# A transformer block on one core: the order of two steps on GpSimd, and the output projection of the first chunk in three pieces

## The chip, the cores and the metric

The kernel runs on one core of one Trainium2 chip. The metric is the device time of one execution in microseconds; the lower the better. The engines are TensorE (PE), VectorE (DVE), ScalarE (ACT), GpSimd (POOL) and SyncE (SP, which here only issues DMAs). Each works through its own instructions in order and waits on semaphores for the others.

## The reference

One block of a diffusion transformer: 2 sequences of 2048 tokens, width 576, 16 heads of 36, hidden width 2304, all in float32.

```python
mod = swish(c) @ w_mod + b_mod
sh_msa, sc_msa, g_msa, sh_mlp, sc_mlp, g_mlp = split(mod, 6, axis=1)
xn = _ln(x) * (1 + sc_msa) + sh_msa
q, k, v = heads(xn @ w_qkv + b_qkv)
q, k = _ln(q, g_q), _ln(k, g_k)                 # over the 36 of a head
attn = softmax(q @ k.T * HD ** -0.5)
x = x + g_msa * (heads_joined(attn @ v) @ w_proj + b_proj)
xn2 = _ln(x) * (1 + sc_mlp) + sh_mlp
x = x + g_mlp * (gelu(xn2 @ w1 + b1) @ w2 + b2)
```

## The kernel before, in words

Products are split: a float32 operand is kept as a 16-bit high part and a 16-bit rest, and a product is the sum of three 16-bit ones.

**Attention.** The work is 8 groups `G` of 4 heads (4 groups for each sequence), each of 16 units `u`; `U = 16 G + u` counts them. A unit is one head and 512 queries, and has 8 steps `s` of 256 keys. In a step PE computes `scores` (L1183) into a PSUM pair, ACT takes the exponential (L755) into one of 4 buffers `p`, and three steps later PE multiplies by the values: `sums` (L1200, float32) for steps 0 to 3, `sums_high` (L1211) and `sums_low` (L1220) for steps 4 to 7. For those DVE first rounds `p` (`round_p`, L927) and forms the rest (`low_p`, L935). `scores` of step s waits for the exponential of step s - 2. So in step 3 of a unit, PE can't begin before ACT has done the exponential of step 1.

**Tiles of the next group.** While a unit is attended, the queries, keys and values of one tile (128 tokens) of the next group are made: PE multiplies 7 of the 14 products in step 0 and 7 in step 1 (`tile_products`, L1237). ACT squares the result in step 4 (L725), DVE sums the squares in step 5 (`tile_sum`, L895, L899), POOL takes the power -1/2 (`tile_power`, L623), and DVE scales by it at the start of the next unit (`tile_normal`, L903).

**Slices of the weights of groups 2 and 3.** The weights `w_qkv` of these two groups are centred and cut during groups 0 and 1. It is done in 6 slices for each of the two, slice `u - 1` in unit `u` = 1 to 6:
- DVE, step 3 of unit u: `sum_word` (L304, a sum for each head);
- POOL, unit u: `centre_word`, two instructions (L311 the mean, L313 the subtraction);
- ACT, unit u + 1, step 0, behind the exponential: `high_word` (L319; L321 and L322 for slice 4; L325 and L326 for slice 5);
- DVE, unit u + 1, step 2: `low_word` (L283).

POOL's loop over the units holds, in this order: `head` (in every fourth unit: copies of the values of the next head, L613, L614 and L616), `centre_word`, `tile_power` for tile U + 1.

**The last group.** In group 7 there is no next group. Its units have `scores` and `sums` only, and the MLP's first chunk of 512 tokens is begun in them. In units 9 to 12 PE multiplies the attention output of one tile each by `w_proj` (`tensor_early`, L1843): 14 products, each of two matmuls of 288 columns, into PSUM banks that nothing else uses there. `PROJECT_AT` says for each step which of the 14 are done in it. DVE takes the result in step 7 of the same unit (`gate_part`, L1731). After the attention come 8 chunks of the MLP (L1864, L1883, L1890), with PE on a fixed order.

Of the kernel before, what the change touches and what calls it, by code (L numbers as in the profile page):

```python
# [340 lines left out]
def split_products(xhi, xlo, w, tokens, cols, bias=True):  # L341

    for k in range(KF):
        yield xhi[:, k, tokens], w[:, k, cols]
        yield xhi[:, k, tokens], w[:, KF + k, cols]
        yield xlo[:, k, tokens], w[:, k, cols]
    yield xhi[:, KF, tokens], w[:, 8, cols]
    if bias:
        yield xlo[0:97, KF, tokens], w[0:97, 9, cols]
    else:  # L350
        yield xlo[:, KF, tokens], w[:, 8, cols]


def attention_mlp(nc, keep, place, x, c, w_mod, b_mod, w_qkv, b_qkv, g_q, g_k, b2, sums_dram, den_dram, rden_dram, mods_dram, out, halves,
# [3 lines left out]
    with ExitStack() as ctx:  # L358
# [3 lines left out]
        TILES = (GROUPS - 1) * NT  # L362
# [111 lines left out]
        def _(sp):  # L474
# [6 lines left out]
            def turn_heads(m):  # L481
                t, i0, i1, _, n = PARTS[m]
                sp.wait_ge(low_ready, m + 1)
                sp.wait_ge(high_ready, 2 * m + 2)
                for i in range(i0, i1):
                    sp.dma_start_transpose(qk_even[:, :, (t * TPC + i) * P:(t * TPC + i + 1) * P],  # L486
                                           stk[:, t % 2, i, :, :].rearrange("p e n -> p (e n)")).then_inc(tq_stored[n], 16)
# [113 lines left out]
        def _(pool):  # L601
            def head(Hh):

                part, h, a = (Hh // GH) % 2, Hh % GH, Hh % 2
                if Hh == 0:
                    pool.wait_ge(raw_ready, RAWS)
                    pool.wait_ge(v_blank, 1)
                else:
                    pool.wait_ge(exp_done, (Hh * NCH - 1) * STEPS + 3)
                if Hh >= 2:  # L610
                    pool.wait_ge(low_p_used, (Hh - 1) * NCH * SPLITS)
                rows = v32[:, part * NT + 2 * SPLIT[0]:part * NT + 2 * SPLIT[-1] + 2, h, :]
                pool.tensor_copy(vr[:, a, :, 0:RW], rows).then_inc(v_high, 1)  # L613
                pool.tensor_copy(v16[:, a, :, :], rows)  # L614
                pool.wait_ge(v_high, Hh + 1)
                pool.tensor_tensor(vr[:, a, :, HP:HP + HD], rows[:, :, 0:HD], vr[:, a, :, 0:HD].bitcast(F32), ALU.subtract).then_inc(head_ready, 1)  # L616

            def tile_power(X):
                if X in EPS_BY_POOL:
                    pool.wait_ge(t_ssq, X + 1)  # L620
                    pool.tensor_tensor(tssq[:, 1, :], tssq[:, 0, :], keep.head_eps[:, 0:QK], ALU.add).then_inc(t_msq, 1)
                pool.wait_ge(t_msq, X + 1)
                pool.tensor_tensor(tssq[:, 1, :], tssq[:, 1, :], keep.power[:, 0:QK], ALU.pow).then_inc(t_rstd, 1)  # L623
# [51 lines left out]
            for U in range(GROUPS * UNITS):  # L675
                G, u = U // UNITS, U % UNITS
                if U == RSTD_IN * UNITS:
                    pool.wait_ge(n_mv, NT + 1)
                    pool.tensor_tensor(nrstd[:, 0, :], nmv[:, :, 1], keep.eps[:, 0:1].broadcast_to([P, NT]), ALU.add).then_inc(n_var, 1)
                    pool.wait_ge(n_var, 1)  # L680
                    pool.tensor_tensor(nrstd[:, 1, :], nrstd[:, 0, :], keep.power[:, 0:NT], ALU.pow).then_inc(n_rstd, 1)
                if (G in HAT_GROUPS and u == 0) or (G == HATS_IN and u == LATE_FROM):
                    n = 2 if G > HATS_IN else int(u == LATE_FROM)
                    pool.wait_ge(n_rows, 16 * (1, 3, 4)[n])
                    if n < 2:
                        pool.memset(hat_lo[n][:, H:KC * P], 1.0)
                    pool.tensor_scalar(scale_row[n], scale_row[n], 1.0, None, ALU.add).then_inc(n_hole, 1)
                if u % NCH == NCH - 1 and U + 1 < SPLIT_UNITS:
                    head(U // NCH + 1)
                if start.slice_at(G, u):  # L690
                    start.centre_word(pool, *start.slice_at(G, u))
                if U + 1 < TILES:
                    tile_power(U + 1)
                if G == GROUPS - 1:
                    rest.gpsimd_early(pool, u)
            rest.gpsimd(pool)
# [700 lines left out]
class Mlp:  # L1397
# [6 lines left out]
    TILES = (B * NG - 1) * NT  # L1404
# [5 lines left out]
    SUMS_AT = {2: 2, 4: 3, 5: 4}  # L1410
    HIGH_IN = MULTIPLY_IN
    PROJECT_IN = {9 + i: i for i in range(TPC)}
    PROJECT_AT = (None, (0, 14), None, None, None, None, None, None)
    NORMAL_IN = {10 + i: i for i in range(TPC)}
    TURN_IN = 14
    TURN_AT, AFFINE_AT, LOW_X_AT = ({s: k for k, s in enumerate(at)} for at in ((0, 1, 3, 4, 6), (1, 2, 4, 5, 7), (2, 3, 5, 6)))
# [412 lines left out]
    def tensor_early(self, pe, u, s):  # L1829
        if u in self.PROJECT_IN and self.PROJECT_AT[s]:  # L1830
            i, (n0, n1) = self.PROJECT_IN[u], self.PROJECT_AT[s]
            ops = list(split_products(self.ohi, self.olo, self.wp, slice(i * P, (i + 1) * P), slice(0, H)))
            if n0 == 0:
                if i == 0:
                    pe.wait_ge(self.olo_ready, KC)
                    pe.wait_ge(self.wp_loaded, 16 * 7)
                    pe.wait_ge(self.ends.t_yn, self.TILES + 1)
                else:
                    pe.wait_ge(self.pair_taken, i)
            for n in range(n0, n1):  # L1840
                l, w = ops[n]
                for half in range(2):
                    last = self.nc.tensor.matmul(self.early_pair[:, half, :], l, w[:, half * HALF:(half + 1) * HALF],  # L1843
                                                 start=(n == 0), stop=(n == len(ops) - 1))
            if n1 == len(ops):
                last.then_inc(self.pair_ready, 1)
        if u == self.TURN_IN and s in self.TURN_AT:
            if s == 0:
                pe.wait_ge(self.pair_taken, TPC)
            self.turn_y(pe, 0, (self.TURN_AT[s],))  # L1850
# [155 lines left out]
```

## Time and profile before

| | |
|---|---|
| median of 3 runs | 2650.73 us (2650.32 to 2651.53) |
| profiled execution | 2651.53 us, of which 2649.7 are the span |
| granted clock of PE | 0.999 |
| busy: PE, DVE, ACT, POOL | 99%, 62%, 55%, 18% |
| a unit in groups 0 to 6 | 12.46 us |
| a unit in group 7, without and with a projection | 10.35 and 14.01 us |

The span is from the first to the last instruction; the time also holds what lies around it. A share of busy time is an average over stages that differ: what a change is worth depends on who waits for whom in its own stage. The starts of instructions on POOL are more to be trusted than their durations.

### The profile page before, as it was taken

The numbers are of one execution on the slowest core, as the hardware profiler recorded it, in microseconds if no ns is written. First come the engines' busy times: TensorE is split into PE (matmuls) and PEld (weight loads), VectorE is DVE, ScalarE is ACT, GpSimd is POOL, SyncE is SP. The second block draws the span as 40 slices with busy tenths as digits, with TensorE's granted clock in tenths as the row PEclk, the third lists the DMA queues.
The fourth block names the chain that finished last, engine by engine and source line by source line (L and its number), as shares of the span: only waits on it lengthen the run. The fifth ranks groups of instructions, "written<-read, shape, count | busy, mean of one in ns | idle before, by whom it ended". The sixth has DMA issues, their size and how long they took to land.

```text
span 2649.7 us, 42010 instructions
## 1 busy us (share of the span) xinstructions
PE 2611.8 (99%) x15820; PEld 1318.7 (50%) x15820; DVE 1647.1 (62%) x2677; ACT 1467.4 (55%) x2174; POOL 469.4 (18%) x339
## 2 busy tenths in 40 slices
PE   6999999999999999999999999999999999999999
PEld 3444444444444444444444334375757575666657
DVE  7788887788888788888888512344343535353421
ACT  4787787777777788788788786412121211111110
POOL 2532332222222222222222100110101010010100
PEclk9999999999999999999999999999999999999999
DMA  7513311133332123333333322402020211202000
GB/s 234 95 36 79 79 36 35 46 74 72 69 73 50 46 70 81 73 78 81 78 79 84 99 77 91 157 15 96 18 79 26 70 60 37 72 24 84 13 19 19
DMA packets 257862, 179.10 MB, mean 68 GB/s; under 512 B 172745, under 2 KB 211087, under 8 KB 256953
## 3 DMA queue, kind: packets, MB, share of 16 engines
q1 hardware_dynamic: 257370, 176.37, 25.0%
q8 instruction: 125, 2.05, 0.3%
q14 instruction: 79, 0.65, 0.1%
q10 hardware_dynamic: 288, 0.04, 0.0%
HBM read 96.49 MB, written 41.06 MB: 52 GB/s over the span
## 4 chain that ended last, share of the span: by engine, by line
PE 94%; DMA 1%; DVE 1%; SPq 1%; ACT 1%; issue 1%; POOL 0%; DVEq 0%; ACTq 0%
PE at_ps L1864 19%; PE at_ps L1200 18%; PE at_ps L1183 17%; PE at_ps L1890 14%; PE at_ps L1237 11%; PE at_ps L1211 8%; PE at_ps L1220 4%; PE at_ps L1883 1%; PE at_ps L1826 1%; PE at_ps L1843 1%; DMA ml_held<-head_rden 1%; PE at_ps L1261 1%; PE at_ps L1918 0%; DMA st_wm_first<-in_L_cond_b_mod 0%; SPq L486 0%
## 5 line engine op out<-in xcount | busy, mean ns | idle before, releaser
L755 ACT ACTIVATE at_p<-at_ps 128x1024 f32<-128x1024 f32 x1024 | 1040.0, 1029 | 330.9 <-PE at_ps L1183 326.3
L1200 PE MATMUL at_ps<-at_p,at_v 128*37 128x512 f32 x2304 | 590.3, 592 | 0.0
L935 DVE TENSOR_TENSOR at_rest_of_p<-at_p,at_pr 128x1024 bf16<-128x1024 f32 x448 | 553.0, 1234 | 15.4
L623 POOL TENSOR_TENSOR at_tssq<-at_tssq,power 128x8 f32<-128x8 f32 x112 | 276.7, 2470 | 880.6 <-DVE at_tssq L899 879.9
L1864 PE MATMUL at_ps<-ml_w2s,ml_hid 128*128 128x288 f16 x3348 | 414.9, 286 | 0.0
L1890 PE MATMUL at_ps<-ml_xhi,ml_w 128*128 128x512 f16 x1296 | 382.0, 379 | 0.0
L1864 PEld LDWEIGHTS at_ps<-ml_w2s,ml_hid 128*128 128x128 f16 x3348 | 327.5, 98 | 82.0
L1211 PE MATMUL at_ps<-at_pr,at_vr 128*101 128x512 f32 x896 | 365.1, 489 | 1.3 <-DVE at_pr L927 1.2
L927 DVE CAST at_pr<-at_p 128x1024 fp32r<-128x1024 f32 x448 | 314.6, 702 | 81.0 <-ACT at_p L755 78.9
L1183 PE MATMUL at_ps<-at_qk_even 109*64 109x512 f16 (+1 forms) x1536 | 308.7, 382 | 3.8 <-ACT at_p L755 2.6
L1183 PE MATMUL at_ps<-at_qk_odd 109*64 109x512 f16 (+1 forms) x1658 | 308.6, 381 | 0.3 <-ACT at_p L755 0.3
L1237 PE MATMUL at_ps<-at_wq,at_xhi 128*128 128x432 f16 x1008 | 295.9, 348 | 0.0
L1653 ACT ACTIVATE ml_g<-at_ps,ml_b1col 128x512 f32<-128x512 f32 x144 | 95.9, 685 | 351.5 <-PE at_ps L1883 244.4
L1731 DVE TENSOR_TENSOR ml_part<-at_ps,ml_gates 128x576 f32<-128x576 f32 x63 | 47.7, 757 | 360.0 <-PE at_ps L1864 333.8
L1183 PEld LDWEIGHTS at_ps<-at_qk_odd 109*64 109x64 f16 (+1 forms) x1658 | 96.9, 107 | 256.0 <-issue 217.6
L1636 ACT ACTIVATE ml_aff<-at_ps,cols 128x512 f32<-128x512 f32 x40 | 31.0, 775 | 348.0 <-PE at_ps L1826 348.0
L1890 PE MATMUL at_ps<-ml_xlo,ml_w 128*128 128x512 f16 x576 | 218.3, 379 | 0.0
L1183 PEld LDWEIGHTS at_ps<-at_qk_even 109*64 109x64 f16 (+1 forms) x1536 | 92.2, 106 | 244.6 <-issue 194.9
L1890 PEld LDWEIGHTS at_ps<-ml_xhi,ml_w 128*128 128x128 f16 x1296 | 123.4, 98 | 158.1 <-issue 16.2
L1200 PEld LDWEIGHTS at_ps<-at_p,at_v 128*37 128x37 f32 x2304 | 134.8, 114 | 119.5 <-issue 1.9
L1237 PE MATMUL at_ps<-at_wq,at_xlo 128*128 128x432 f16 (+1 forms) x560 | 193.9, 346 | 0.0
L1787 DVE CAST ml_hid<-ml_g 128x512 f16<-128x512 f32 x144 | 61.2, 425 | 205.0 <-ACT ml_g L1653 205.0
(189 smaller groups left out, 2365.3 us busy)
## 6 DMA issues: line engine op xcount, KB each, us to landing
head_sums<-at_oT SPq DMA_DIRECT2D x256, 72.0 KB
ml_held<-head_sums SPq DMA_DIRECT2D x64, 256.0 KB
at_xy<-in_L_cond_w SPq DMA_DIRECT2D x34, 288.0 KB
w_halves<-at_wq SPq DMA_DIRECT2D x68, 144.0 KB
at_xy<-in_x SPq DMA_DIRECT2D x32, 288.0 KB, 2.8
ml_x<-in_x SPq DMA_DIRECT2D x8, 1152.0 KB, 5.4
out<-ml_x SPq DMA_DIRECT2D x7, 1152.0 KB, 4.5
ml_held<-head_rden SPq DMA_DIRECT2D x24, 216.0 KB
```

Source lines behind the costliest of these rows:

```text
L623: pool.tensor_tensor(tssq[:, 1, :], tssq[:, 1, :], keep.power[:, 0:QK], ALU.pow).then_inc(t_rstd, 1)
L755: act.activation(p[:, s % NP, :], ps[:, 2 * (s % 2):2 * (s % 2) + 2, :].rearrange("p a n -> p (a n)"), ACT.Exp).then_inc(exp_done, 1)
L927: nc.vector.tensor_copy(pr[:, n % NZ, :], p[:, s % NP, :]).then_inc(rounded, 1)
L935: nc.vector.tensor_tensor(rest_of_p[:, n % NL, :], p[:, s % NP, :], pr[:, n % NZ, :].bitcast(F32), ALU.subtract).then_inc(low_p_ready, 1)
L1183: last = nc.tensor.matmul(ps[c:c + keys, 2 * (s % 2) + a, :], qk[0:SW, GH + h, key:key + keys], qk[0:SW, h, qc * CH:(qc + 1) * CH], start= ...
L1200: last = nc.tensor.matmul(acc[a * HP:a * HP + RW, bank_of(U)], v32[:, (G % 2) * NT + 2 * s + a, h, :], p[:, s % NP, a * CH:(a + 1) * CH], ...
L1211: last = nc.tensor.matmul(acc[0:VW, bank_of(U)], vr[:, Hh % 2, 2 * k + a, :], pr[:, n % NZ, a * CH:(a + 1) * CH], start=False, stop=False, ...
L1220: last = nc.tensor.matmul(acc[a * HP:a * HP + RW, bank_of(U)], v16[:, Hh % 2, 2 * k + a, :], rest_of_p[:, n % NL, a * CH:(a + 1) * CH], st ...
L1237: last = nc.tensor.matmul(tile_bank(X, 0, 3 * GW), l, rhs[:, g * 3 * GW:(g + 1) * 3 * GW], start=(n == 0), stop=(n == count - 1))
L1653: act.activation(self.g32[:, f % 2, :], self.up_bank(f), ACT.Gelu_apprx_tanh, bias=self.b1col[:, f:f + 1], scale=1.0 / WS).then_inc(self.g ...
L1864: last = nc.tensor.matmul(self.pair(i)[:, half, :], l, w[:, half * HALF:(half + 1) * HALF], start=(n == 0), stop=(n == len(ops) - 1))
L1890: last = nc.tensor.matmul(self.up_bank(f), w, xs, start=first and n == 0, stop=not first and n == len(ops) - 1)
```

## The change

It has two parts that have nothing to do with each other. On POOL, `tile_power` of a unit stands ahead of `centre_word` of the same unit, where it stood behind. `PROJECT_AT` gives 5, 5 and 4 of the 14 products to steps 1, 2 and 3, where it gave all of them to step 1.

```diff
                 if u % NCH == NCH - 1 and U + 1 < SPLIT_UNITS:
                     head(U // NCH + 1)
+                if U + 1 < TILES:
+                    tile_power(U + 1)
                 if start.slice_at(G, u):
                     start.centre_word(pool, *start.slice_at(G, u))
-                if U + 1 < TILES:
-                    tile_power(U + 1)
                 if G == GROUPS - 1:
                     rest.gpsimd_early(pool, u)
...
     PROJECT_IN = {9 + i: i for i in range(TPC)}
-    PROJECT_AT = (None, (0, 14), None, None, None, None, None, None)
+    PROJECT_AT = (None, (0, 5), (5, 10), (10, 14), None, None, None, None)
     NORMAL_IN = {10 + i: i for i in range(TPC)}
```

## Rows read from the trace of the kernel before

**Rows 1.** The page: the chain that ended last, by engine

```profile
PE 94%; DMA 1%; DVE 1%; SPq 1%; ACT 1%; issue 1%; POOL 0%; DVEq 0%; ACTq 0%
```

**Rows 2.** By stretch: length, busy PE, PEld, DVE, ACT, POOL, clock, DMA

```profile
111.13:211.00 99.87, 99.87 (x563) 42.82 (x561) 83.40 (x124) 79.98 (x121) 30.52 (x26) 1.00 0.23 52
...
1588.57:1644.50 55.93, 55.93 (x370) 24.95 (x368) 10.80 (x22) 34.15 (x37) 2.20 (x6) 1.00 0.34 107
```

**Rows 3.** Waits of PE's matmuls, 111.2 to 1500 us: total, times, longest

```profile
PE at_ps L1211 <- DVE at_pr L927: 1.2, 2, 0.7
PE at_ps L1183 <- ACT at_p L755: 0.3, 1, 0.3
```

**Rows 4.** The chain in order of time, unit 3: start, us, what

```profile
138.69 0.47 PE at_ps L1211 x2
139.16 1.29 PE at_ps L1237 x7
140.46 0.43 PE at_ps L1183 x2
```

**Rows 5.** Timeline of PE and ACT, units 3 and 6: start, us, [idle before]

```profile
141.28 0.62 PE L1183 MATMUL at_ps<-at_qk_even 109*64 109x512 f16 x4
...
137.45 0.56 ACT L319 ACTIVATE at_wq<-st_later 128x432 f16<-128x432 f32 x1
138.73 1.02 ACT L755 ACTIVATE at_p<-at_ps 128x1024 f32<-128x1024 f32 x1 [0.71 <-PE at_ps L1183]
140.93 1.02 ACT L755 ACTIVATE at_p<-at_ps 128x1024 f32<-128x1024 f32 x1 [1.17 <-PE at_ps L1183]
...
175.40 0.56 ACT L322 ACTIVATE st_later<-st_later 64x432 f16<-64x432 f32 x1
176.10 1.02 ACT L755 ACTIVATE at_p<-at_ps 128x1024 f32<-128x1024 f32 x1
```

**Rows 6.** Timeline of POOL: units 0 to 3

```profile
110.77 1.64 POOL L623 TENSOR_TENSOR at_tssq<-at_tssq,power 128x8 f32<-128x8 f32 x1 [6.77 <-DVE at_tssq L899]
119.94 0.73 POOL L311 TENSOR_SCALAR st_lone_mean<-st_lone 128x8 f32<-128x8 f32 x1 [7.53 <-DVE st_lone L304]
120.76 1.60 POOL L313 TENSOR_TENSOR st_later<-st_later,st_lone_mean 128x288 f32<-128x288 f32 x1
...
131.99 0.25 POOL L311 TENSOR_SCALAR st_lone_mean<-st_lone 128x8 f32<-128x8 f32 x1 [4.64 <-DVE st_lone L304]
132.32 0.67 POOL L313 TENSOR_TENSOR st_later<-st_later,st_lone_mean 128x288 f32<-128x288 f32 x1
137.31 2.52 POOL L623 TENSOR_TENSOR at_tssq<-at_tssq,power 128x8 f32<-128x8 f32 x1 [4.32 <-DVE at_tssq L899]
139.41 0.68 POOL L613 CAST at_vr<-at_v 128x296 fp32r<-128x296 f32 x1
```

**Rows 7.** Timeline of DVE: units 1 and 2

```profile
119.88 0.69 DVE L927 CAST at_pr<-at_p 128x1024 fp32r<-128x1024 f32 x1
...
132.34 1.20 DVE L927 CAST at_pr<-at_p 128x1024 fp32r<-128x1024 f32 x1 [0.44 <-ACT at_p L755]
...
139.10 0.69 DVE L927 CAST at_pr<-at_p 128x1024 fp32r<-128x1024 f32 x1
139.82 1.34 DVE L935 TENSOR_TENSOR at_rest_of_p<-at_p,at_pr 128x1024 bf16<-128x1024 f32 x1
```

**Rows 8.** Timeline of ACT and PE at the start of the attention

```profile
100.61 2.84 ACT L755 ACTIVATE at_p<-at_ps 128x1024 f32<-128x1024 f32 x3
...
102.59 0.62 PE L1183 MATMUL at_ps<-at_qk_even 109*64 109x512 f16 x4 [0.23 <-ACT at_p L755]
```

**Rows 9.** The chain in order of time: group 7, and a long run of the MLP

```profile
1589.86 3.54 PE at_ps L1843 x28
1593.40 0.55 PE at_ps L1183 x4
...
1765.01 13.23 PE at_ps L1864 x108
```

## The prediction

> **What bounds the kernel now.** I read the page first, then the busy times by stretch, then the chain of work that ended last in the two places that the change touches, and last the timelines of ACT, DVE and POOL there. The page gives PE 94% of the chain that ended last [rows 1]. That is a mean over the whole span, so the two stages come next: in the first 100 us of the group 0 stage PE is busy in all of its 99.87 us, and in the part of group 7 with the projections in all of 55.93 [rows 2]. A matmul's end is modelled, so I don't take this alone. The table of waits says the same from the other side: from 111 to 1500 us a matmul waited 1.2 us for DVE and 0.3 us for ACT, all told [rows 3]. The chain through unit 3 shows no piece that isn't PE, and each piece begins where the last ended [rows 4]. So whatever holds PE up in these stages is added to the time in full, and nothing that only lightens ACT, DVE or POOL is worth anything.
>
> **Part A: the order on POOL.** In units 1 to 6 of groups 0 and 1, POOL now runs `centre_word` and then `tile_power`; afterwards it is the other way round. Twelve slices of weights are centred there. No instruction is added. What matters is what each waits for. `centre_word` waits for DVE's sum of step 3 (L304); `tile_power` waits for DVE's L899, which comes in step 5 and, since DVE runs behind, only after ACT has begun the next unit. Behind `centre_word` waits ACT's `high_word`, in step 0 of the next unit and ahead of the exponentials of steps 1, 2 and so on.
>
> Take unit 3 (PE's step 1 block at 139.16). Its slice was centred from 131.99 to 132.99, and ACT took it at 137.45 [rows 5, 6]: 4.5 us to spare. Turned round, the centring can't start before the power is through, and the power started at 137.31, only 0.14 us before ACT wants the result. POOL's next instruction after it starts 2.10 us later (139.41 after 137.31) [rows 6]; I use this spacing, not the recorded 2.52 us.
>
> - A small gain first. The DVE rounding of step 4 (L927) takes 1.20 us when the centring (L313 at 132.32) falls on it and 0.69 us otherwise [rows 6, 7]. With the centring moved away, L899 and the power come 0.50 us earlier: 137.31 becomes 136.81.
> - Where the centring lands: 2.10 us after the power's start. DVE then runs the rounding of step 7 (L927, from 1.79 to 2.48 us after that start) and the subtraction L935 (from 2.51) [rows 7]. One case of this kind is in the trace, the first slice: L311 started 0.06 us into an L927, took 0.73 us instead of 0.25, and L313 after it took 1.60 instead of 0.67 [rows 6, 7]. From the end of the L927 (120.57) to the end of L313 (122.36) it took 1.79 us. So I take 2.48 + 1.79 = 4.27 us after the power's start: the slice is centred at 141.08.
> - ACT: 0.05 us for the semaphore (estimate, from the 0.04 us between the end of the scores at 138.69 and the exponential at 138.73 [rows 4, 5]), 0.70 us for `high_word` with what follows it (the same 0.56 us activation at 175.40 has the exponential behind it at 176.10 [rows 5]), then the exponential of step 1, 1.02 us: it ends at 142.85 where it ended at 139.75.
> - PE: `scores` of step 3 waits for that exponential. It started at 141.28. An ACT end reaches PE in about 0.06 us (exponentials from 100.61, the second of three ends near 102.53, matmul at 102.59 [rows 8]). So it starts at 142.91: PE stands still for 1.63 us.
>
> From the second stalled unit on there is 0.19 us more. From the exponential of step 2 to that of step 4 ACT works without a gap. Before, the exponential of step 2 started 0.35 us ahead of PE's scores of step 3 (140.93, 141.28 [rows 5]). After a stall it starts 0.10 us ahead of the end of the step 1 exponential (three in a row overlap by 0.10 each: 2.84 us, not 3.06 [rows 8]), and the scores 0.06 behind that end, 0.16 apart: ACT is 0.19 us later against PE. DVE's L899 follows the exponential of step 4, and so the next power. That gives 1.82 us. For the last two slices of a group `high_word` is two activations of 0.56 us [rows 5], so 2.38 us. A group: 1.63 + 3 x 1.82 + 2 x 2.38 = 11.85 us; two groups 23.7 us. Nothing later gives this back, since PE is the chain from there on. The rest that hangs on it has cover: the head's copies on POOL come behind the centring in one unit, but are wanted only in step 7 of the next, and `low_word` on DVE waits for the exponential of step 2, which ends later than `high_word`.
>
> The trace gives both ends of this cost. Below: if the centring runs freely 2.10 us after the power (0.32 from L311 to L313, and 0.67 for it [rows 6]: 3.09 instead of 4.27), each stall is 1.18 us shorter: 0.45, 0.64, 1.20, or 9.5 us in all. Were the power as short as the one of 1.64 us in unit 0 [rows 6], another 0.46 us goes and the sum is 4.0 us. Above: without the 0.50 us gain on DVE it is 29.7 us. I take 23.7, because the one slice of the trace that starts inside an L927 behaved so, and 2.10 lies 0.3 us inside that window at either side.
>
> The Trainium skill (SBUF — State Buffer, Who interferes with whom) states that a DVE instruction in a two-port mode, or with two SBUF inputs against a GpSimd instruction that reads SBUF, shares a port pair with GpSimd, that whoever issues first holds it for the whole instruction, and that the other blocks. The stretched pairs of [rows 6, 7] agree with this. By issue order alone L313, 2.42 us after the power, would come 0.09 us ahead of L935 at 2.51 and run freely, which is the sum of 9.5 us; with L311 first held by the L927, it is the sum of 23.7 us.
>
> **Part B: the projection in three pieces.** In units 9 to 12 of group 7, 14 products of two matmuls each stood in step 1; now 5, 5 and 4 stand in steps 1, 2 and 3. The matmuls are the same 112. ACT gets no new scores during the long block, but PE is the bound: it is busy throughout this stretch [rows 2], and no piece of its chain is late [rows 9]. The block takes 3.54 us, of which 28 x 0.1225 = 3.43 are its matmuls, by the rate of the same form in a long run, 13.23 us for 108 [rows 9]; the scores behind it take 0.55 us and not the 0.43 that they take in a chain without a change [rows 4, 9]. So entering and leaving a block costs 0.11 + 0.12 = 0.23 us. Eight more entries cost 1.8 us. Bounds: nothing, if the 7-product blocks of the earlier groups are the model, with scores of 0.43 us behind them [rows 4], to 2.6 us, if a block costs 0.33. The shorter gap on ACT is worth nothing, as no matmul waited for it. The result is read by DVE in step 7; after step 3 it still is there in time, four steps ahead.
>
> **Sum.** The profiled execution took 2651.53 us: 2649.7 of span and 1.8 around it. It is the slowest of the three; the median is 2650.73. 2651.5 + 23.7 + 1.8 = 2677.0, and by the median 2676.2. I forecast 2676.5.
>
> **Rivals.**
> - *The centring runs freely* (9.5 us in A): 2650.7 + 9.5 + 1.8 = 2662. For it: L313 would start 0.09 us ahead of L935. Against it: L311 starts inside an L927. Chance 0.15.
> - *More than that*: the stall feeds itself, or the 0.50 us don't come: 2650.7 + 29.7 + 1.8 = 2682 and beyond. For it: DVE is busy 83% of this stretch [rows 2]. Against: by the working above DVE has no new wait. Chance 0.13, a third of it above 2684.
> - *Nothing happens*, because ACT has more slack than I count or power and centring overlap: 2651 to 2653. The exponential of step 1 waited 0.71 us [rows 5] and the scores of step 3 stand 1.5 us behind its end, a slack of some 2.2 us against a lateness of 3.7. Chance 0.04.
> - *Faster*: if ACT never has to wait for the centring, the 0.50 us of DVE in 12 units would be the one effect, and would shorten the time where DVE sets the pace: 12 x 0.50 = 6 us less, 2650.7 - 6.0 + 1.8 = 2646.5. It decides from the point where the centring ends before ACT's 137.45 and PE waits for DVE; PE waited for DVE 1.2 us in 1400 [rows 3]. Chance 0.02.
>
> **How the numbers follow.** The forecast has 0.66, so some 0.94 lie on the slower side by more than 0.2% (5.3 us, about what can be told from no change here). The rival of 9.5 us and B come to 11.3 us, beyond that; the lowest bound, 4.0 and B, comes to 5.8. Same: 0.04; faster: 0.02. The range takes in the freely running centring and the sum without the DVE gain: 2661 to 2684.
>
> **What the profile after would show.** Right: the matmuls of step 3 (L1183) in units 2 to 7 and 18 to 23 wait for ACT, some 1.6 to 2.4 us each, 12 times, where none did; `high_word` (L319 and its neighbours) waits for POOL L313, some 3.7 us; L311 and L313 come after the power with 0.7 and 1.6 us; units there take 14.1 to 14.8 us and not 12.46; L927 of step 4 is 0.69 us. In group 7 three blocks of some 1.3, 1.3 and 1.1 us stand in each unit with a projection, each with scores of 0.55 us behind it and no wait of PE; the unit is 0.46 us longer. Wrong: L313 at 0.67 us and stalls near 0.6 us (the first rival), stalls that grow from slice to slice (the second), or ACT's L319 with no wait (the third). A granted clock below 1.00 in the stalled units would add what I haven't counted; it was 1.00 in both stretches [rows 2].

## The result and the profile after

The changed kernel takes 2684.51 us (median of 4 runs, 2684.31 to 2687.15), the kernel before takes 2651.13 us beside it (2650.32 to 2653.14, 4 runs). The ratio is 1.0127, with a 95% interval of 1.0109 to 1.0145: 33 us slower. The direction is as forecast. The time is 8 us above the forecast of 2676.5 and 0.5 us outside the range of 2661 to 2684. The profiled execution took 2684.21 us, 2682.4 of them span, at a mean granted clock of 0.996 (before: 2649.7 and 0.999).

The chain that ended last, by engine, over the whole span after the change:

```profile
PE 87%; issue 5%; POOL 2%; DVE 2%; DMA 1%; ACT 1%; SPq 1%; DVEq 0%; POOLq 0%; ACTq 0%
```

It was 94% of PE before [rows 1]. The 5% of "issue" are a sign of the new loop: where PE stands still the chain goes back over POOL, from one power to the next.

**Where PE waits.** The table of waits of the kernel after: first PE's, from 111 to 436 us (groups 0 and 1 where slices are centred), then ACT's behind POOL. The columns are what waited, for what, the microseconds in all, how many times and the longest.

```profile
PE at_ps L1183 <- ACT at_p L755: 23.0, 12, 2.5
...
ACT at_wq L319 <- POOL st_later L313: 32.0, 8, 4.1
...
ACT at_wq L321 <- POOL st_later L313: 7.8, 2, 4.1
ACT at_wq L325 <- POOL st_later L313: 7.4, 2, 3.7
```

There are twelve stalls of the scores, as forecast; before, PE had waited 0.3 us for ACT in 1400 us [rows 3]. Behind them `high_word` waits for the centring twelve times, some 4 us each. So the place and the mechanism of part A are there.

**One stalled unit.** The timeline of unit 3 (start, duration, engine, line; in brackets the idle time before and what ended it), on POOL, DVE, ACT and PE, to be read beside [rows 5 to 7]:

```profile
138.96 2.52 POOL L623 TENSOR_TENSOR at_tssq<-at_tssq,power 128x8 f32<-128x8 f32 x1 [9.73 <-DVE at_tssq L899]
141.56 1.23 POOL L311 TENSOR_SCALAR st_lone_mean<-st_lone 128x8 f32<-128x8 f32 x1
142.88 0.67 POOL L313 TENSOR_TENSOR st_later<-st_later,st_lone_mean 128x288 f32<-128x288 f32 x1
...
134.49 0.69 DVE L927 CAST at_pr<-at_p 128x1024 fp32r<-128x1024 f32 x1 [0.44 <-ACT at_p L755]
...
141.47 1.23 DVE L935 TENSOR_TENSOR at_rest_of_p<-at_p,at_pr 128x1024 bf16<-128x1024 f32 x1
...
143.58 0.56 ACT L319 ACTIVATE at_wq<-st_later 128x432 f16<-128x432 f32 x1 [4.05 <-POOL st_later L313]
144.05 1.92 ACT L755 ACTIVATE at_p<-at_ps 128x1024 f32<-128x1024 f32 x2
...
126.83 0.36 PE L1237 MATMUL at_ps<-at_wq,at_xhi 128*128 128x432 f16 x1
...
140.97 0.36 PE L1237 MATMUL at_ps<-at_wq,at_xhi 128*128 128x432 f16 x1
...
155.29 0.36 PE L1237 MATMUL at_ps<-at_wq,at_xhi 128*128 128x432 f16 x1
```

The rounding of step 4 (L927 at 134.49) takes 0.69 us, so the 0.50 us on DVE came as forecast. L311 starts 2.60 us after the power, not 2.10. It meets the subtraction L935, which began 0.09 us before it, and ends with it; L313 then runs freely in 0.67 us. The slice is centred 4.59 us after the power's start (forecast 4.27). ACT begins `high_word` 0.03 us later, and the exponential is 0.47 us behind it (forecast 0.70). In all the exponential comes 5.09 us after the power, where 5.02 were forecast: the two errors nearly cancel. The last three lines are the first matmul of the tile block of step 1 in units 2, 3 and 4. From 126.83 to 140.97 are 14.14 us for a unit with the first stall, which is 12.46 + 1.68 (forecast 1.63). From there to 155.29 are 14.32 us: + 1.86 (forecast 1.82).

**What isn't a wait.** PE waits 23.0 us there, but groups 0 and 1 have become longer by 30.3. The chain gives the block of the first tile products of unit 1 and of unit 8 in group 0, and of units 16 and 24, which stand ahead of and behind the stalls of group 1 (start, duration, engine, line, count):

```profile
114.53 1.29 PE at_ps L1237 x7
...
216.84 1.30 PE at_ps L1237 x7
...
316.51 1.30 PE at_ps L1237 x7
...
431.37 1.30 PE at_ps L1237 x7
```

From 114.53 to 216.84 are 102.31 us for 7 units; at 12.46 us each they would be 87.22, so group 0 pays 15.1 us. From 316.51 to 431.37 are 114.86 us for 8 units instead of 99.68: 15.2 us. The windows of the kernel after (stretch, length, then busy us of PE, PE's loads, DVE, ACT and POOL with counts, granted clock, DMA share, GB/s) show where part of it went:

```profile
138.50:152.85 14.35, 12.56 (x71) 5.32 (x70) 10.53 (x17) 9.83 (x17) 5.97 (x6) 1.00 0.14 31
167.20:182.40 15.20, 13.40 (x68) 5.28 (x66) 10.13 (x16) 9.11 (x16) 4.42 (x3) 0.89 0.13 27
182.40:198.80 16.40, 14.24 (x72) 5.76 (x70) 10.62 (x17) 10.63 (x17) 4.43 (x3) 0.90 0.12 26
175.00:176.00 1.00, 1.00 (x4) 0.18 (x2) 0.42 (x1) 1.00 (x3) 0.00 (x0) 0.50 0.08 16
```

The first window is a stalled unit at full clock. The two others of its kind have 0.89 and 0.90, and inside the first of them the microsecond from 175 to 176 has 0.50, which is the lower level, 1.2 GHz. (Before, no stretch between 111 and 436 us was below 1.00.) PE's timeline says what that does to its matmuls:

```profile
173.75 0.80 PE L1183 MATMUL at_ps<-at_qk_even 109*64 109x512 f16 x4 [1.80 <-ACT at_p L755]
174.34 1.92 PE L1200 MATMUL at_ps<-at_p,at_v 128*37 128x512 f32 x4
176.05 1.07 PE L1183 MATMUL at_ps<-at_qk_even 109*64 109x512 f16 x4
```

After a gap of 1.80 us the four scores take 0.80 us, not 0.62, the four of the sums 1.92, not 1.03, and the four scores behind them 1.07, not 0.60: about half speed. Cut finer, the trace has four such stretches, at the stalls that end at 173.75, 190.13, 403.24 and 419.36, each 3.4 us long at 0.50. Three begin within 1 us of PE's return to work, the one at 403.24 half a microsecond before it. Each of them can cost at most 1.7 us; the account with filled gaps below gives 1.3. The Trainium skill (TensorE: Matmul & The Clock Gate, The HAM clock gate) says that PE's clock is gated by how busy it has been of late; the row with 0.50 behind a stall agrees.

**Part B.** The chain through a unit with a projection in group 7:

```profile
1620.04 1.33 PE at_ps L1843 x10
1621.37 0.55 PE at_ps L1183 x4
1621.92 0.86 PE at_ps L1200 x4
1622.78 1.33 PE at_ps L1843 x10
...
1625.53 1.09 PE at_ps L1843 x8
...
1634.49 1.33 PE at_ps L1843 x10
```

These are the pieces of 1.3, 1.3 and 1.1 us with scores of 0.55 us behind them that the prediction named. The unit takes 1634.49 - 1620.04 = 14.45 us instead of 14.01: 0.44 us, and 1.8 us for four. PE waits for nothing in this stretch.

### The profile page after: what moved, and what is told of

The parts are those of the page before. It is cut to its first block, busy times and chain, and to the rows that moved or that the text cites. A ratio compares the mean times of both kernels' runs of the same rounds, so it can differ in the third digit from the quotient of the medians.

```text
span 2682.4 us, 42010 instructions
## 1 busy us (share of the span) xinstructions
PE 2621.9 (98%) x15820; PEld 1318.4 (49%) x15820; DVE 1642.9 (61%) x2677; ACT 1467.1 (55%) x2174; POOL 474.8 (18%) x339
## 4 chain that ended last, share of the span: by engine, by line
PE 87%; issue 5%; POOL 2%; DVE 2%; DMA 1%; ACT 1%; SPq 1%; DVEq 0%; POOLq 0%; ACTq 0%
PE at_ps L1864 19%; PE at_ps L1200 17%; PE at_ps L1183 16%; PE at_ps L1890 14%; PE at_ps L1237 9%; PE at_ps L1211 7%; PE at_ps L1220 3%; POOL at_tssq L623 1%; PE at_ps L1883 1%; PE at_ps L1826 1%; PE at_ps L1843 1%; POOL st_lone_mean L311 1%; DMA ml_held<-head_rden 1%; PE at_ps L1918 0%; DMA st_wm_first<-in_L_cond_b_mod 0%
## 5 line engine op out<-in xcount | busy, mean ns | idle before, releaser
L935 DVE TENSOR_TENSOR at_rest_of_p<-at_p,at_pr 128x1024 bf16<-128x1024 f32 x448 | 552.1, 1232 | 15.4
L927 DVE CAST at_pr<-at_p 128x1024 fp32r<-128x1024 f32 x448 | 309.2, 690 | 85.5 <-ACT at_p L755 83.4
L1183 PE MATMUL at_ps<-at_qk_even 109*64 109x512 f16 (+1 forms) x1536 | 309.8, 383 | 15.0 <-ACT at_p L755 13.9
L1183 PE MATMUL at_ps<-at_qk_odd 109*64 109x512 f16 (+1 forms) x1658 | 309.9, 383 | 11.8 <-ACT at_p L755 11.7
L1237 PE MATMUL at_ps<-at_wq,at_xhi 128*128 128x432 f16 x1008 | 295.9, 348 | 0.0
L1183 PEld LDWEIGHTS at_ps<-at_qk_odd 109*64 109x64 f16 (+1 forms) x1658 | 96.5, 107 | 266.1 <-issue 214.0
L1183 PEld LDWEIGHTS at_ps<-at_qk_even 109*64 109x64 f16 (+1 forms) x1536 | 92.3, 106 | 257.2 <-issue 192.9
L1237 PE MATMUL at_ps<-at_wq,at_xlo 128*128 128x432 f16 (+1 forms) x560 | 193.9, 346 | 0.0
L1211 PEld LDWEIGHTS at_ps<-at_pr,at_vr 128*101 128x101 f32 x896 | 149.8, 167 | 77.7 <-DVE at_pr L927 2.8
```

What stands on the lines that cost most here:

```text
L927: nc.vector.tensor_copy(pr[:, n % NZ, :], p[:, s % NP, :]).then_inc(rounded, 1)
L935: nc.vector.tensor_tensor(rest_of_p[:, n % NL, :], p[:, s % NP, :], pr[:, n % NZ, :].bitcast(F32), ALU.subtract).then_inc(low_p_ready, 1)
L1183: last = nc.tensor.matmul(ps[c:c + keys, 2 * (s % 2) + a, :], qk[0:SW, GH + h, key:key + keys], qk[0:SW, h, qc * CH:(qc + 1) * CH], start= ...
L1211: last = nc.tensor.matmul(acc[0:VW, bank_of(U)], vr[:, Hh % 2, 2 * k + a, :], pr[:, n % NZ, a * CH:(a + 1) * CH], start=False, stop=False, ...
L1237: last = nc.tensor.matmul(tile_bank(X, 0, 3 * GW), l, rhs[:, g * 3 * GW:(g + 1) * 3 * GW], start=(n == 0), stop=(n == count - 1))
```

## The experiments

The questions were: do the two parts add up to the whole; is the missing time the clock or more waiting; what on POOL sets the size of a stall; and where does the stall go if its cause is met elsewhere. Each kernel is compared with runs of the kernel before made beside it, as a ratio. The median of these was 2652.32 us (16 runs) for the order alone, the three pieces alone, seven filled matmuls and the late high part; 2651.29 (19 runs) for the seven pieces, the nearly full gaps, the control and the mean ahead of the power; 2651.72 (15 runs) for the copy, the odd units and both parts late.

### Each part alone

The new order on POOL with the old projection:

```diff
-                if start.slice_at(G, u):
-                    start.centre_word(pool, *start.slice_at(G, u))
                 if U + 1 < TILES:
                     tile_power(U + 1)
+                if start.slice_at(G, u):
+                    start.centre_word(pool, *start.slice_at(G, u))
```

> The new order on POOL alone, with the projection in one block. My theory: all of the loss but 1.8 us is here, made of 12 stalls of PE behind ACT (1.7, then 1.9, and 2.4 us for the last two slices of a group, 24 us in all) and of stretches after some of the stalls in which the granted clock is 0.5 (6 to 7 us in all, in the profile after in units 5 and 6 of group 0 and in unit 6 of group 1). So 2651.1 + 24 + 6.5 = 2681.6 to 2683 us, with a granted clock under 1.00 in some stalled units. Rival 1: the two parts add up to more than each, and alone the order costs what was forecast: 2651.1 + 23.7 = 2674.8 us, clock 1.00. Rival 2: the clock falls only by chance in the runs of the changed kernel, and the times of this one scatter between 2675 and 2683.

Measured: 2684.57 us (4 runs, 2683.96 to 2685.56), ratio 1.0126 [1.0109, 1.0142], clock 0.994 to 0.996. This is the whole of the loss, as near as it can be told. PE waits 22.9 us twelve times, as after. Over the same units as above group 0 pays 16.6 us and group 1 15.3, with a granted clock of 0.96 and 0.97 over 125 us of each. Here one unit had a lower clock that had none in the kernel after (0.88 from 124.40 to 138.50, behind the first stall). So what is lost to the clock isn't fixed to certain stalls. This trace has five low stretches of 3.4 us where the kernel after had four. In the profiled executions that is 1.6 us, enough to hide the 1.8 us of part B, and the result lies above the 2681.6 to 2683 that were expected.

The old order with the projection in three pieces:

```diff
-    PROJECT_AT = (None, (0, 14), None, None, None, None, None, None)
+    PROJECT_AT = (None, (0, 5), (5, 10), (10, 14), None, None, None, None)
```

> The projection in three pieces alone, with the old order on POOL. My theory: eight more entries into a block at 0.23 us, 2651.1 + 1.8 = 2652.9 us, no wait of PE in group 7, pieces of 1.33, 1.33 and 1.09 us. Rival: the part of the loss that wasn't forecast, 7 to 8 us, is here, through what the shorter gap does to ACT and DVE: 2660 us.

Measured: 2654.23 us (10 runs, 2651.29 to 2655.45), ratio 1.0008 [0.9998, 1.0017]. The time alone doesn't settle a cost of 1.8 us; the unit of 14.46 us in its trace does, four times 0.45. Some of the scatter is the clock: in this trace PE waits 2.15 us for DVE in the MLP, to 1738.03, and its clock is low for 3.4 us behind that. The trace of the kernel before has the same wait, 2.26 us to 1736.99, at 1.00.

And in seven pieces of two products, to make the disputed cost larger:

```diff
-    PROJECT_AT = (None, (0, 14), None, None, None, None, None, None)
+    PROJECT_AT = (None, (0, 2), (2, 4), (4, 6), (6, 8), (8, 10), (10, 12), (12, 14))
```

> The kernel before with the projection in seven pieces of two products, in steps 1 to 7. Each piece but the first adds an entry into a block: 24 of them. At 0.23 us each 5.5 us: 2652.3 + 5.5 = 2657.8 us; a piece takes 4 x 0.1225 + 0.11 = 0.60 us. At the upper bound of 0.33 us it is 7.9 us, 2660. If an entry costs nothing, 2652.

Measured: 2657.49 us (10 runs, 2654.83 to 2660.0), ratio 1.0025 [1.0016, 1.0035], which is 6.6 us. A piece of its chain and the scores behind it:

```profile
1590.73 0.60 PE at_ps L1843 x4
1591.33 0.55 PE at_ps L1183 x4
```

The piece is 0.60 us where four of its matmuls are 0.49 (4 x 0.1225), and the scores are 0.55, not 0.43: 0.11 + 0.12 us again. A unit takes 15.36 us (the first piece of the next unit comes at 1604.08 where this one's stood at 1588.72), 1.35 more than 14.01 for six more entries. So the 24 entries cost 5.4 us by the trace, 0.22 to 0.23 us each, and the price per entry holds at three times the number. The 6.6 us of the times agree with that, as their interval runs from 4.2 to 9.3 us.

### Stalls filled with matmuls: is it the clock?

If only the waiting for ACT cost time, matmuls put into the gaps could at best cost nothing. If the clock costs as well, they make the kernel faster, although they are more work. Seven matmuls on data that are already there, into a bank that is free, ahead of the scores of step 3, in the six stalled units of each group:

```diff
+                    if G in (0, 1) and 2 <= u <= 7 and s == 3:
+                        pe.wait_ge(t_yn, U + 2)
+                        for n in range(7):
+                            nc.tensor.matmul(tile_bank(U, 0, 3 * GW), xhi[:, n % KF, 0:P], wq[:, n % KF, 0:3 * GW], start=True, stop=True)
                     scores(G, U, h, qc, s)
```

> The new order on POOL alone, and in each of the 12 stalled units PE does 7 more matmuls of 432 columns (1.3 us) just before the scores of step 3, into a PSUM bank that is free there; nothing reads what they give. They lie inside the stall of 1.7 to 2.4 us. If the clock falls because PE stands still in the stalls, it now stays at 1.00, and the time is lower although work was added: 2651.1 + 24 = 2675 us, some 7 below the same kernel without them. If the loss beyond the forecast is anything else (DVE, POOL or ACT being late), the time stays at 2682 or rises, up to 2698 if the 12 x 1.3 us aren't hidden.

Measured: 2679.43 us (4 runs, 2674.66 to 2680.7), ratio 1.0108 [1.0091, 1.0125], with clocks of 0.997 to 0.999. The intervals of this and of the order alone overlap, so the times by themselves don't decide it. The trace does, in the execution of 2674.66 us (the other three, of which there is no trace, took 2678.99 to 2680.7 at 0.997 and 0.998, so it seems, though no trace shows it, that seven matmuls don't keep the clock up in every execution; 2675 had been expected): PE's waits, its chain at units 1 and 8, a stalled unit on PE, and the window.

```profile
PE at_ps L1183 <- ACT at_p L755: 8.5, 12, 1.2
...
113.25 1.29 PE at_ps L1237 x7
...
213.01 1.30 PE at_ps L1237 x7
...
141.88 1.45 PE L1339 MATMUL at_ps<-at_wq,at_xhi 128*128 128x432 f16 x7
143.84 0.62 PE L1183 MATMUL at_ps<-at_qk_even 109*64 109x512 f16 x4 [0.50 <-ACT at_p L755]
...
111.00:236.00 125.00, 120.74 (x676) 51.80 (x675) 92.38 (x146) 89.13 (x135) 35.05 (x27) 1.00 0.21 49
```

PE still waits for ACT in each of the twelve units, so the arrival of the exponential sets their length and the seven matmuls cost nothing. The clock is 1.00. From 113.25 to 213.01 are 99.76 us: the group pays 12.54 us (the other 12.55), not 15.1. So the stalls themselves are 25.1 us, and 30.3 - 25.1 = 5.2 us of the profile after are what PE's slower clock adds behind them, 1.3 us for each of the four low stretches. (The order alone has five: 31.9 - 25.1 = 6.8 us, 1.4 each.)

With more matmuls, so that nearly all of each gap is full:

```diff
-                        for n in range(7):
+                        for n in range(9 if u <= 5 else 12):
```

> As the run with 7 more matmuls in each stalled unit, now 9 in the first four stalled units of a group and 12 in the last two, so that PE stands still for some 0.2 to 0.5 us only in a stall of 1.7 to 2.7 us. If the clock falls because PE stands still, it falls no more in any of the runs: granted clock as in the runs of the kernel before (0.996 to 0.999), and the time is the forecast without a clock, 2652 + 25.1 = 2677 us, every run within 2 us of it, though 30 matmuls were added again. If instead 0.3 to 0.5 us of the time of a stalled unit follows from the added work, it is above the 2679.4 us of 7 matmuls.

Measured: 2675.38 us (4 runs, 2674.63 to 2678.28), ratio 1.0091 [1.0075, 1.0106], clocks of 0.998 and 0.999, where 2677 was expected. PE waits for ACT six times, 1.6 us in all, and each group pays 12.58 us, as with seven, at a clock of 1.00. These are 120 matmuls more than the order alone (36 more than with seven, not the 30 of the expectation), and 0.35% less in the ratio to the kernel before: some 9 us, between two intervals that only just don't overlap, so the size is known far worse than the sign. That the length of a group doesn't move by more work in the gaps (12.54 and 12.58 us), while the time comes down where the clock stays up, shows the second cost apart from the first.

The control is the kernel before with the seven matmuls of the first of these two:

> The kernel before, with the same 7 added matmuls in the same 12 units. No stall covers them there. A block of 7 takes 1.29 us and some 0.1 to 0.2 us to enter: 12 x 1.45 = 17 us, 2652 + 17 = 2669 us. This is the control of the filled runs: if the added matmuls cost nothing here either, the filled runs say nothing on the stalls.

Measured: 2671.28 us (4 runs, 2667.53 to 2672.56), ratio 1.0074 [1.0058, 1.0089]. Its trace has 9.41 us more in group 0, 1.57 for each block. The added matmuls are real work that costs time where there is no gap to take them; in the stalled units they were free.

### What sets a stall on POOL

The mean (L311) ahead of the power, so that only the subtraction L313 stays behind it:

```diff
         pool.tensor_scalar(self.lone_mean[:, :], self.lone[:, :], 1.0 / HD, None, ALU.mult).then_inc(self.w_mean, 1)
+
+    def centre_rest(self, pool, n, i):
...
         pool.wait_ge(self.w_mean, m + 1)
...
                 if start.slice_at(G, u):
                     start.centre_word(pool, *start.slice_at(G, u))
                 if U + 1 < TILES:
                     tile_power(U + 1)
+                if start.slice_at(G, u):
+                    start.centre_rest(pool, *start.slice_at(G, u))
```

> The new order on POOL alone, but only the subtraction (L313) stands behind the power; the mean (L311) stands ahead of it, where it was. In the changed kernel L311 starts 2.61 us after the power and is held 1.23 us, to the end of DVE's L935 of step 7, and L313 ends 4.59 us after the power. Theory of the shared port: L313 now starts at 2.61, during that L935, is held until it ends at 3.74 and ends at 4.25 to 4.3, with a duration of 1.6 to 1.7 us; each stall is 0.3 us shorter, 4 us in all, and since stalls are shorter the clock may fall less: 2680 to 2676 us. Rival: it isn't held by DVE but only follows the power; then it takes 0.67 us, ends at 3.3 and each stall is 1.3 us shorter, 16 us in all: 2664 us.

Measured: 2657.51 us (9 runs, 2654.65 to 2659.42), ratio 1.0022 [1.0012, 1.0032]. Both numbers that were expected missed. PE waits 5.4 us, ten times, the clock is 1.00, and group 0 pays 3.1 us. The timeline of unit 3, POOL and then DVE (lines below the new ones are 3 to 5 higher: L316 is the subtraction of L313, L940 is L935):

```profile
137.90 2.52 POOL L626 TENSOR_TENSOR at_tssq<-at_tssq,power 128x8 f32<-128x8 f32 x1 [4.57 <-DVE at_tssq L904]
140.01 0.90 POOL L316 TENSOR_TENSOR st_later<-st_later,st_lone_mean 128x288 f32<-128x288 f32 x1
...
140.41 1.57 DVE L940 TENSOR_TENSOR at_rest_of_p<-at_p,at_pr 128x1024 bf16<-128x1024 f32 x1
```

The subtraction starts 2.11 us after the power, inside DVE's rounding of step 7 (0.90 us and not 0.67), and ends 3.01 after it. It was ahead of DVE's subtraction, and now that is the one that is held, 1.57 us and not 1.23. Of the 33 us of the new order some 6 are left with L311 out of the way: most of the loss hangs on when the first instruction behind the power starts and on who comes first.

The other way to ask: leave L311 behind the power, as in the new order, but make it a copy (this leaves out the division by 36, so the centring takes off the sum and not the mean):

```diff
-        pool.tensor_scalar(self.lone_mean[:, :], self.lone[:, :], 1.0 / HD, None, ALU.mult).then_inc(self.w_mean, 1)
+        pool.tensor_copy(self.lone_mean[:, :], self.lone[:, :]).then_inc(self.w_mean, 1)
```

> The new order on POOL alone, with the small instruction L311 as a copy and not a multiplication by 1/36, so the centring subtracts 36 times too much: this changes what the kernel computes. The question is why L311 starts 2.61 us after the power when L613 (a copy) and L313 alone (a subtraction) start after 2.10 us. If it is the kind of the instruction, the copy starts at 2.10 us, inside DVE's L927, and L313 gets in ahead of DVE's L935 or behind it, and ends at 3.1 or 4.3 us and not 4.59: stalls shorter by 1.5 or 0.3 us, 2666 or 2680 us. If it is the place behind the power in this program (the two waits on semaphores in front of it), nothing moves: 2.61 us and 2684 us.

Measured: 2676.04 us (4 runs, 2674.59 to 2678.9), ratio 1.0089 [1.0073, 1.0104]. POOL in unit 3:

```profile
138.54 2.52 POOL L623 TENSOR_TENSOR at_tssq<-at_tssq,power 128x8 f32<-128x8 f32 x1 [9.74 <-DVE at_tssq L899]
140.61 0.47 POOL L311 COPY st_lone_mean<-st_lone 128x8 f32<-128x8 f32 x1
141.17 1.64 POOL L313 TENSOR_TENSOR st_later<-st_later,st_lone_mean 128x288 f32<-128x288 f32 x1
```

The copy starts 2.07 us behind the power, inside an L927, and L313 is stretched to 1.64 us and ends 4.27 us after the power, the forecast's figure. So that working was right for an instruction that may start at 2.1 us. A copy and a TENSOR_TENSOR do; the TENSOR_SCALAR of the kernel starts at 2.60, after the power's recorded end. Why the kinds differ is open. PE waits 20.2 us here (22.9 with the order alone), with clocks of 0.97 and 0.99 in the two groups. The time is 4 us below the 2680 that were expected for this case; the trace, of the execution of 2678.9 us, has three low stretches where the order alone has five.

The new order in odd units only, three in each group, so that each stall stands by itself:

```diff
+                late = u % 2 == 1
-                if start.slice_at(G, u):
+                if start.slice_at(G, u) and not late:
                     start.centre_word(pool, *start.slice_at(G, u))
                 if U + 1 < TILES:
                     tile_power(U + 1)
+                if start.slice_at(G, u) and late:
+                    start.centre_word(pool, *start.slice_at(G, u))
```

> The new order on POOL in units 1, 3 and 5 of groups 0 and 1 alone, the old one in 2, 4 and 6. Six stalls, each after a unit without one. By the forecast's working, the 0.19 us that a stall adds is handed on only by a stall right before it, so each of the first two of a group is 1.63 to 1.68 us, as the first of a group was, and not 1.86; the third, with two activations, 2.5. That is 5.9 us a group, 11.7 in all, plus what the clock takes: 2651.5 + 11.7 = 2663.2 us at a clock of 1.00, up to 2666 if it falls after single stalls too. If the lateness isn't handed on but comes with each stall, 2 x (1.86 x 2 + 2.7) = 12.8 us.

Measured: 2664.01 us (5 runs, 2661.78 to 2667.35), ratio 1.0045 [1.0031, 1.0058]. PE waits six times, 11.0 us in all. Units 1 and 8 on the chain (L1240 is L1237 of the kernel before):

```profile
115.33 1.29 PE at_ps L1240 x7
...
208.26 1.29 PE at_ps L1240 x7
```

These are 92.93 us: group 0 pays 5.7, where 5.9 were expected: 1.68, 1.66 and 2.38 us by its blocks of step 1. The 0.19 us from stall to stall is indeed handed on only by a stall right before. Group 1 pays 7.4 us, with a clock of 0.99 in its window, one low stretch. Six of twelve stalls cost 12 us of the 33.

### The consumer moved as well

If the lateness is the whole cause, the new order should cost nothing once ACT takes the slice later. `high_word` in step 2 and `low_word` in step 4:

```diff
-                    if s == 0 and start.slice_at(G, u, 1):
+                    if s == 2 and start.slice_at(G, u, 1):
...
-                    if s == 2 and start.slice_at(G, u, 1):
+                    if s == 4 and start.slice_at(G, u, 1):
```

> The new order on POOL alone, but ACT cuts the high part of a slice behind the exponential of step 2, not of step 0, and DVE its low part in step 4, not 2. If all of the loss comes from ACT waiting for the centring ahead of the exponential of step 1, nothing is left: 2651 +- 1 us, no matmul waits for ACT. DVE still gains 0.5 us in each of the 12 units (the rounding of step 4 at 0.69 us); if that were worth anything, up to 6 us less: 2645. Rival: the order on POOL costs by itself, through the centring or the head's copies that come later: over 2660 us.

Measured: 2658.91 us (7 runs, 2657.66 to 2659.78), ratio 1.0027 [1.0015, 1.0038]. The twelve stalls of 1.6 to 2.5 us are gone (the waits of PE from 111 to 436 us):

```profile
PE at_ps L1211 <- DVE at_pr L927: 1.2, 4, 0.3
PE at_ps L1183 <- ACT at_p L755: 0.9, 4, 0.2
```

But 2651 was expected and 7 us are lost, 3.5 in each group. Three units of a group take 12.78 us (the power stands at 135.78 and at 148.56), 0.3 more than PE needs. `low_word` (L283, 0.61 us) now stands ahead of the rounding of step 4 on DVE, and so ahead of everything that leads to the next power; DVE sets the pace. So DVE is busy 83% of the time [rows 2] but has hardly a place where 0.6 us are free. The larger part is in the two units with two activations: they take 13.75 us, 1.3 more each. There L321 still waits 0.28 us for the centring in step 2, and with L322 behind it the exponential of step 3 comes late. With `low_word` at the beginning of DVE's step 3:

```diff
-                    if s == 0 and start.slice_at(G, u, 1):
+                    if s == 2 and start.slice_at(G, u, 1):
...
+                    if s == 3 and start.slice_at(G, u, 1):
+                        start.low_word(dve, *start.slice_at(G, u, 1))
                     if tail and s == 3:
                         tile_low(U)
...
-                    if s == 2 and start.slice_at(G, u, 1):
-                        start.low_word(dve, *start.slice_at(G, u, 1))
```

> The new order on POOL alone, ACT cuts the high part behind the exponential of step 2, and DVE the low part at the start of its step 3, where it stands still for 1.8 us waiting for ACT, not in step 4 ahead of the rounding, where it made the run with the late high part lose 0.3 us in a unit. If DVE's queue ahead of the rounding of step 4 was what that run lost by (3.5 us a group, 7 in all), all of it comes back: 2651.5 +- 1 us. If the subtraction and copies on POOL that now fall on DVE's L906 and L935 are what it lost by, 2656 to 2658 stays.

Measured: 2653.44 us (11 runs, 2650.89 to 2655.9), ratio 1.0006 [0.9997, 1.0016]; PE waits for ACT twice, 0.5 us in all. The times alone can't tell this from the kernel before. The trace can: the units with one activation are back at 12.46 us, so the queue of DVE was the cause of their 0.3 us, but the two units with two activations take 12.77 and 13.16 us, which is 1.0 us a group and 2.0 in all. So the order on POOL costs 2 us and not 33 when its consumer comes two steps later. It brings nothing either: PE had no gap there to win back. No kernel here beat the kernel before.

## Why the prediction was right and where it failed

- **The bound** was read rightly: all of what was added to PE's chain in the two stages came out in the time.
- **Part A, the mechanism**: right in its place (L1183 of step 3), its number (12) and its chain (power, centring, `high_word`, exponential, scores). The order alone gives the loss as a whole, and all but 2 us of it goes when `high_word` and `low_word` are moved.
- **Part A, the first four stalls**: 1.68 and 1.86 us against 1.63 and 1.82. This is partly luck. The centring ended 4.59 us after the power and not 4.27, because L311, a TENSOR_SCALAR, starts 2.60 us behind the power and then is held by L935; the prediction took 2.10, the spacing of another kind of instruction [rows 6]. Against that the exponential came 0.47 us behind the start of `high_word` and not 0.70. The Trainium skill (SBUF — State Buffer, Who interferes with whom) lets whoever issues first hold the shared port; all three orders that the runs show agree (L935 first: L311 1.23 us; L313 first: L940 1.57; L935 first: L313 1.64).
- **Part A, the last two stalls**: 2.56 and 2.72 us, where the prediction had 2.38. This is from the trace with filled gaps, where no clock disturbs: the blocks of step 1 of units 6, 7 and 8 start 15.02 and 15.18 us apart, behind a stalled unit of 14.33; the kernel before has 12.46 there. ACT's timeline of slice 4 in the kernel after shows why:

```profile
187.90 0.56 ACT L321 ACTIVATE at_wq<-st_later 64x432 f16<-64x432 f32 x1 [3.71 <-POOL st_later L313]
188.47 0.56 ACT L322 ACTIVATE st_later<-st_later 64x432 f16<-64x432 f32 x1
189.05 1.94 ACT L755 ACTIVATE at_p<-at_ps 128x1024 f32<-128x1024 f32 x2
```

  The exponential comes 1.15 us behind L321, 0.68 more than the 0.47 behind a single L319. There the exponential overlaps the activation ahead of it by 0.09 us; here neither L322 nor the exponential overlaps what is ahead of it (0.57 and 0.58 us apart). These 0.68 are about the 0.69 us by which 15.02 exceeds 14.33. The 0.16 us more of the last stall come with a power that starts later against PE, 1.86 us ahead of the block where it was 2.01. In all, the stalls without the clock are 25.1 us and not 23.7; 1.0 of the 1.4 us are these four.
- **The step that failed is the sum**: "2651.5 + 23.7 + 1.8 = 2677.0" has no term for the clock. The last paragraph named a clock below 1.00 as something it hadn't counted and took the 1.00 of the two stretches before [rows 2] as the value after. But that 1.00 was read where PE never stopped, and the change is one that makes it stop. The trace of the kernel before had a place where PE stops, in its first 50 us: PE waits 2.52 us for DVE, to 35.91, and behind that its clock is at 0.50 for 6.8 us.

```profile
34.00:50.00 16.00, 13.39 (x65) 7.95 (x66) 14.75 (x35) 7.91 (x13) 3.00 (x4) 0.79 1.03 385
```

  The missing term is 5.2 us in the profile after, and about 9 us between the medians of the order alone and of the one with nearly full gaps. The 8.0 us between forecast and median are these 5.2, the 1.4 of the stalls, 0.6 that weren't followed, 0.5 by which the forecast stands below its own sum, and 0.3 between the profiled execution and the median. Without the 5.2 us of the clock the result would lie inside the range. The upper bound had been taken from another cause, the missing gain of 0.50 us on DVE, which didn't occur.
- **Part B**: right to a tenth. 0.44 us a unit, 1.8 us in all, by 0.22 us an entry, which held for 24 entries too. It couldn't have been told from the times of the change alone.
- **The sum by the traces**: 25.1 + 5.2 + 1.8 = 32.1 of the 32.7 us by which the spans differ. The other 0.6 us are small differences elsewhere and weren't followed: the block of unit 1 stands at 114.53 and not 114.24 (0.3 more), from unit 24 to the first projection the kernel after is 0.4 faster, and the MLP is 0.7 longer.
- **The rivals**: the freely running centring came half true (L313 ran in 0.67 us), but behind an L311 that had lost the time already. A stall that feeds itself didn't come: equal stalls follow each other with 1.86 us. The second rival (2682 and beyond) had the right size of time by the wrong cause: the 0.50 us on DVE did come. The third and fourth, nothing and faster, didn't come.

Open: why one stall brings the clock down and the next doesn't (the unit at 138.50 stayed at 1.00 with a stall of 1.79 us, and the one behind the stall of 1.80 at 173.75 fell), and why a TENSOR_SCALAR starts later behind a power than a copy does.

## What to carry to other kernels

When a change puts new gaps into a full TensorE, add a term for the clock behind them, and take it from no stretch in which the engine never paused, but from one of the same trace in which it did; matmuls in the gap that need nothing are a cheap way to measure it. When two instructions of an engine change places, work out for each when its consumer asks for it, and move the consumer before anything else. When the start of an instruction decides which of two engines gets a shared port, take its spacing from an instruction of its own kind, or keep both cases as ends of the range.

## What the runs showed of the hardware that I had not expected

- The granted clock fell to 0.50 (1.2 GHz) at single gaps of 1.8 to 2.5 us in a stream that is otherwise full, for 3.4 us each time, and not at each of them, nor at the same ones in two kernels with the same order on POOL. It happened four times in twelve stalls in the kernel after, five times with the order alone, and at 1.3 to 1.4 us each it cost 5.2 and 6.8 us.
- On POOL a TENSOR_SCALAR of 128x8 starts 2.60 us after the start of a power of 128x8, a copy 2.07 and a TENSOR_TENSOR 2.11, although the power is recorded with 2.52 us in all three.
- Whether L311 or L313 meets DVE's L935, and who is first, moves the end of the centring: it comes 3.01, 4.27 or 4.59 us after the power.
- PE can do some 9 to 12 more matmuls of 432 columns in a stalled unit for nothing, and pays 1.57 us for seven in a full one.
- DVE at 83% had no 0.6 us free ahead of the rounding of step 4: `low_word` there made three units of a group 0.3 us longer.
